# An attention and expert-routing layer on one core: the closing steps of the routing stage move from GpSimd to VectorE, and the closing orders of ScalarE and VectorE are written out

## What is computed

```python
x = x + layernorm(attn(layernorm(x)))     # linear attention: elu(q)+1, elu(k)+1, kv summed over the sequence
x = x + layernorm(ffn(layernorm(x)))

def _moe(x, wg, w1, v1, w2):
    scores = softmax(x @ wg.T)            # 32 experts
    weights, idx = top_k(scores, 8)
    weights = weights / sum(weights)
    # each token's row goes through 8 experts of width 192, and the results are added with their weights
    h = silu(xs @ w1[e]) * (xs @ v1[e])
    out = zeros.at[t_s].add((h @ w2[e]) * w_s)
```

## Time and profile before

| | us |
|---|---|
| median of 3 runs | 2469.23 (2468.17 to 2470.07) |
| profiled execution, its own time | 2465.01 |
| span of the profiled execution, first to last instruction | 2463.3 |
| PE busy in the span | 2234.5 (91%) |
| DVE busy | 1487.0 (60%) |
| ACT busy | 1237.6 (50%) |
| POOL busy | 956.6 (39%) |

### The profile page before, as it was taken

The page is one execution under the profiler, slowest core; times in us unless marked ns, Lnnn a source line. Parts: engine busy times, 40 slices in busy tenths (PEclk is TensorE's granted clock), DMA queues, the critical chain, the costliest instruction groups (busy, mean ns, idle before and its releaser), DMA issues.

```text
span 2463.3 us, 64597 instructions
## 1 busy us (share of the span) xinstructions
PE 2234.5 (91%) x11850; PEld 1922.4 (78%) x11851; DVE 1487.0 (60%) x4836; ACT 1237.6 (50%) x2643; POOL 956.6 (39%) x1128
## 2 busy tenths in 40 slices
PE   7999799999989999995698999989999898989980
PEld 5887488888858888884588988878889787978970
DVE  4555467777767777775555555565554555555546
ACT  3344456666655666663344454555444544454433
POOL 1212015555525555556333333333334333333432
PEclk9999899999999999997799999999999999999995
DMA  3234102333333333333897888888777777777767
GB/s 121 85 120 126 61 26 100 120 118 116 126 127 115 129 108 118 119 130 129 251 225 186 184 205 177 189 197 177 149 154 140 187 154 154 140 170 147 139 110 294
DMA packets 165230, 358.64 MB, mean 146 GB/s; under 512 B 21168, under 2 KB 21168, under 8 KB 165040
## 3 DMA queue, kind: packets, MB, share of 16 engines
q0 software_dynamic: 60512, 144.74, 28.4%
q1 hardware_dynamic: 91216, 173.89, 23.3%
q10 hardware_dynamic: 13440, 39.33, 4.8%
HBM read 178.21 MB, written 179.66 MB: 145 GB/s over the span
## 4 chain that ended last, share of the span: by engine, by line
PE 38%; issue 4%; DMA 3%; ACTq 3%; ACT 2%; DVE 1%; POOL 1%; DVEq 1%; SPq 0%; POOLq 0%
PE bank L465 7%; PE bank L467 6%; PE bank L466 6%; PE bank L456 4%; PE bank L482 3%; PE bank L486 2%; PE bank L475 2%; PE bank L484 2%; PE bank L483 2%; PE bank L485 2%; DMA LATE<-w_in 1%; DMA RAW<-w_in 1%; ACTq L325 1%; POOL sorted_rows L1525 1%; ACT WB L333 1%
## 5 line engine op out<-in xcount | busy, mean ns | idle before, releaser
L1459 POOL DMA_INDIRECT moe_sum<-Y,aidx x276 | 432.1, 1565 | 783.6 <-DMA moe_sum<-Y,aidx 404.0
L929 PE MATMUL bank<-WB,XH 128*128 128x512 f32 x1536 | 477.3, 392 | 0.0
L465 PE MATMUL bank<-WB,XL 128*128 x1104 | 399.5, 362 | 0.0
L467 PE MATMUL bank<-WB,XH 128*128 x1104 | 373.9, 339 | 0.0
L466 PE MATMUL bank<-WB,XH 128*128 x1104 | 372.3, 337 | 0.0
L929 PEld LDWEIGHTS bank<-WB,XH 128*128 128x128 f32 x1536 | 290.7, 189 | 58.3 <-issue 0.5
L929 PE MATMUL bank<-WB,XL 128*128 128x512 f32 x768 | 316.0, 411 | 10.4 <-DVE XL L1241 10.4
L929 PE MATMUL bank<-WB,SH 128*128 128x512 f32 x1024 | 317.3, 391 | 0.0
L709 DVE SCALAR_TENSOR_TENSOR BIG<-BIG,bank x276 | 95.9, 347 | 357.1 <-ACT BIG L527 270.5
L1525 POOL DMA_INDIRECT sorted_rows<-BIG,pos x256 | 265.7, 1038 | 94.6 <-issue 94.6
L527 ACT ACTIVATE BIG<-bank x276 | 91.4, 331 | 346.2 <-PE bank L467 320.3
(11 more groups left out here) (215 smaller groups left out, 4266.8 us busy)
## 6 DMA issues: line engine op xcount, KB each, us to landing
BIG<-sorted_rows SPq DMA_DIRECT2D x278, 274.0 KB
Y<-x_in SPq DMA_DIRECT2D x64, 256.0 KB, 2.8
RAW<-w_in ACTq DMA_DIRECT2D x15, 768.0 KB
LATE<-w_in ACTq DMA_DIRECT2D x15, 768.0 KB
sorted_rows<-BIG SPq DMA_DIRECT2D x33, 274.0 KB
moe_sum<-LATE SPq DMA_DIRECT2D x34, 256.0 KB, 3.0
LATE<-x_in SPq DMA_DIRECT2D x32, 256.0 KB
RAW<-wo_in SPq DMA_DIRECT2D x16, 512.0 KB, 3.5
```

The source lines that it names most:

```text
L465: nc.tensor.matmul(eu[s][:, 0:UP], XL[:, s, k, :], wh, start=k == 0, stop=False)
L467: last = nc.tensor.matmul(eu[s][:, 0:UP], XH[:, s, k, :], wl, start=False, stop=k == KC - 1)
L929: last = nc.tensor.matmul(ps, w, m, start=start and i == 0, stop=stop and i == len(terms) - 1)
L1459: nc.gpsimd.indirect_dma_start(acc_dram[:, :], bass.IndirectOffsetOnAxis(aidx[:, s:s + 1], 0), rows, None, compute_op=ALU.add).then_inc(s_ ...
```

## The change

GpSimd's list behind the last step of b keeps only the power -0.5 of each norm (`root`), the memory for padding (`set_pads`) and the scatters. VectorE does the rest: the residual adds and second norms of tiles 30 and 31, the output norm of tile 31, `pages_needed` for the tiles 29 to 31, and `note_pages` for the tiles 28 to 31. VectorE's and ScalarE's steps from step 32 (VectorE) and 33 (ScalarE) on are written out as `drain()`. Inside the loop nothing changes: there GpSimd still does all of it. `place` is cut in two, `place` and `place_rows`, so that in the closing steps `note_pages` can stand between them. The conversion of expert 0's weights moves: ScalarE's high parts stand behind tile 31's `turned`, and VectorE's low parts stand in `moe_dve`, behind the first part of the table. In `moe_act` the high parts of expert 1 now stand ahead of the load of expert 2.

```diff
+        def pages_needed(eng, t):
...
+            eng.tensor_scalar(need[:, :], carry[:, :], 0.0, None, ALU.is_gt).then_inc(s_need, 1)
+
+        def note_pages(eng, t, s):
...
@@ moe_act
             act.wait_ge(s_ex, TILES)
             nc.scalar.activation(negmax[:, :], mhalf[:, :], ACT.Silu)
+            for piece in range(len(PIECES)):
+                weights_high(act, 1, 1, 1, piece)
             act.wait_ge(s_elo, 1)
             load_weights(act, 2, 0)
-            for piece in range(len(PIECES)):
-                weights_high(act, 1, 1, 1, piece)
@@ moe_dve
             settled()
+            for piece in range(len(PIECES)):
+                weights_low(dve, 0, 0, 0, piece)
             steps = TILES // 4
             dve.wait_ge(s_pad0, 5)
             dve.wait_ge(s_pld, 16)
@@ ScalarE
+            def drain():
+                last = TILES - 1
+                turned(last - 1)
+                row_norm(last, 1)
+                exps(last - 1)
+                turned(last)
+                act.wait_ge(s_q, 4 * TILES)
+                for piece in range(len(PIECES)):
+                    weights_high(act, 0, 0, 0, piece)
+                exps(last)
+                row_out(last - 1, 0)
+                row_out(last, 1)
@@ VectorE
+            def rstd(slot, s_in, s_mid, s_out, n, s_used):
+
+                wait(dve, s_used, n - 1)
+                dve.wait_ge(s_in, n)
+                stand(dve)
+                nc.vector.tensor_scalar(ve[:, slot:slot + 1], mv[:, slot, 1:2], NORM_EPS, None, ALU.add).then_inc(s_mid, 1)
+                dve.wait_ge(s_mid, 2 * n)
+                stand(dve)
+                nc.vector.tensor_scalar(nmr[:, slot:slot + 1], mv[:, slot, 0:1], rs[:, slot:slot + 1], -1.0, ALU.mult,
+                                        ALU.mult).then_inc(s_out, 1)
+
+            def drain():
+                last = TILES - 1
+
+                def second_norm(t, s):
+                    dve.wait_ge(s_on, t + 1)
+                    dve.wait_ge(s_xres[s], (t - s) * 8 + 16)
+                    nc.vector.tensor_tensor(XRES[:, s, :], XRES[:, s, :], on, ALU.add).then_inc(s_x2, 1)
+                    dve.wait_ge(s_x2, t + 1)
+                    mean_var(XRES[:, s, :], 2, s_2bs, s_2mv, t + 1, s_2rs)
+                    rstd(2, s_2mv, s_2ve, s_2rs, t + 1, s_row)
+
+                def take_pages(t):
+                    ranks(t)
+                    pages_needed(dve, t)
+
+                def give_pages(t, s):
+                    place(t, s)
+                    note_pages(dve, t, s)
+                    last_pages(t)
+
+                def give_rows(t, s):
+                    place_rows(t, s)
+                    list_places(t, s)
+
+                scaled_low(4 * TILES - 2, 0)
+                list_places(last - 3, 0)
+                second_norm(last - 1, 0)
+                scaled_low(4 * TILES - 1, 1)
+                note_pages(dve, last - 3, 0)
+                last_pages(last - 3)
+                route(last - 2, 1)
+                take_pages(last - 2)
+                dve.wait_ge(s_o, 4 * TILES)
+                mean_var(po[1][:, :], 1, s_obs, s_omv, TILES, s_ors)
+                rstd(1, s_omv, s_ove, s_ors, TILES, s_on)
+                give_pages(last - 2, 1)
+                give_rows(last - 2, 1)
+                second_norm(last, 1)
+                route(last - 1, 0)
+                take_pages(last - 1)
+                give_pages(last - 1, 0)
+                give_rows(last - 1, 0)
+                route(last, 1)
+                take_pages(last)
+                give_pages(last, 1)
+                give_rows(last, 1)
@@ GpSimd
+            def root(slot, s_mid, n):
+                pool.wait_ge(s_mid, 2 * n - 1)
+                stand(pool)
+                nc.gpsimd.tensor_tensor(rs[:, slot:slot + 1], ve[:, slot:slot + 1], mhalf[:, :], ALU.pow).then_inc(s_mid, 1)
+
             def drain():
                 last = TILES - 1
-                residual(last - 1, 0)
-                rstd(2, s_2mv, s_2ve, s_2rs, last, s_row)
-                note_pages(last - 3, 0)
-                send(last - 3, 0, 0, 3)
-                pages_needed(last - 2)
-                rstd(1, s_omv, s_ove, s_ors, last + 1, s_on)
-                send(last - 3, 0, 3, 5)
-                residual(last, 1)
-                send(last - 3, 0, 5, 7)
-                rstd(2, s_2mv, s_2ve, s_2rs, last + 1, s_row)
-                note_pages(last - 2, 1)
-                send(last - 3, 0, 7, 8)
+                root(2, s_2ve, last)
+                send(last - 3, 0, 0, 5)
+                root(1, s_ove, TILES)
+                send(last - 3, 0, 5, TOP_K)
+                root(2, s_2ve, TILES)
                 set_pads()
-                send(last - 2, 1, 0, 2)
-                pages_needed(last - 1)
...
+                send(last - 2, 1, 0, TOP_K)
+                send(last - 1, 0, 0, TOP_K)
+                send(last, 1, 0, TOP_K)
```

More of the change, by code:

```diff
@@ L1153, in b_body @@
                     if c == 0 and live(t, 3):
[L1154 to L1161 removed]
+                        turned(t - 3)
                     if not fixed or 0 <= j - 2 < 4 * TILES:
@@ L1400, in b_body @@
             def b_body(t, s, b):
                 fixed = isinstance(t, int)
+                if fixed and t >= TILES:
+                    return
                 for c in range(CHUNKS):
@@ L1436, in b_body @@
                         route(t - 3, 1 - s)
-                    if fixed and (t, c) in FIRST_LOW:
-                        for piece in FIRST_LOW[t, c]:
-                            weights_low(dve, 0, 0, 0, piece)
                     if c == 3 and live(t, 3):
                         place(t - 3, 1 - s)
+                        place_rows(t - 3, 1 - s)
             run_b(dve, b_body)
+            drain()
             moe_dve(dve)
```

87 lines of the change are left out of this document (41 added, 46 removed).

## The result

The changed kernel took 2472.03 us in the median of 12 runs (2463.99 to 2479.78), beside 2464.62 for the kernel before (12 runs, 2457.00 to 2470.07). The ratio is 1.003, its 95% interval 1.0015 to 1.0044: 7.4 us, 0.3% slower, where 10.0 us faster (2459.2 us) was predicted, in a range that ended at 2467.5. The profiled execution took 2475.59 us, its span is 2473.3 us, 10.0 longer than before: 3.1 of them lie ahead of the closing steps, 4.1 in them and 2.8 behind them.

The account below looks back on a forecast made before the run. GpSimd's list in the closing steps was taken as the bound, with the table close behind. Earlier last scatter 8.1 plus landing 2.4 gave 10.5, less 0.5 for collisions: 10.0 us off 2469.2, so 2459.2 us, range 2454.5 to 2467.5.

Parts of the forecast that it names:

- the table chain: Closing steps, page list to table: list 11 us earlier, table 20.9 us behind it at 1180.9 or 1181.8, before the landing.
- a first transpose set free by the table: Sign of being wrong: TensorE's first expert transpose released by the table instead of by the scatters.
- the second rival: Closing steps: VectorE's two-input steps hold up GpSimd, or its handover chain becomes the bound; gain 0.9 us, 2468.3; chance 0.13.
- the room for tile 30: VectorE's chain: tile 30's positions ready near 1154, its scatters start at 1159.4, so 5 us of room.
- The slower rival: Experts' part: expert 2's load goes out late and ScalarE waits for it; 6 to 8.5 us slower, 2476; chance 0.05.
- the first rival: Closing steps: landing stays at 6.97 and the unexplained gap stays whole; gain 6.7 us, 2462.5; chance 0.18.
- First scatter: GpSimd's first scatter of tile 28 starts at 1133.0 instead of 1134.08, 1.1 us earlier.
- Stream: GpSimd, first to last scatter: pace 39.9, powers 1.8, padding 1.8, new wait 1.3, half the gap 0.9; 45.7 us.
- The unexplained gap: GpSimd, behind the first scatter: 2.11 us, 1.8 above the usual; half of that, 0.9, was taken to stay.
- Collisions: Closing steps: GpSimd slowed beside VectorE instructions with two SBUF inputs; 0.5 us put off the gain.
- Landing: Last scatter, start to landing: 4.6 us instead of 6.97 with one rival weight load less, 2.4 us gained.
- the case I had set beside the sum and not used: Last scatter: engines go round queues with work, so the landing stays near 6.97 and the sum is 8.1 us.

Follow-up runs that it names:

- e1: The changed kernel run again unaltered: 2454.47 us against 2463.50 for the kernel before, ratio 0.9973.
- e2: Changed kernel with expert 2's load ahead of the high parts of expert 1 again: 2456.17 us against 2463.50 for the kernel before, ratio 0.9981.
- e14: The changed kernel run again unaltered in a later set: 2462.59 us against 2465.05 for the kernel before, ratio 0.9995.
- e3: Changed kernel with VectorE's low parts of expert 0 ahead of tile 31's last row steps again: 2457.85 us against 2463.50 for the kernel before, 0.9979.
- e10: Changed kernel with expert 2's load issued only behind the first transposes: 2461.75 us against 2464.89 for the kernel before, 0.9989.
- e6: Changed kernel with both weight moves undone (expert 2's load, low parts of expert 0): 2454.91 us, 0.9946 of the kernel before.
- e4: Changed kernel with six GpSimd memsets as pauses between the scatters of tiles 29 to 31: 2458.75 us against 2463.50 for the kernel before, 0.998.
- e16: Changed kernel with six memsets of 0.5 us between the scatters of tiles 29 to 31: 2458.96 us against 2465.11 for the kernel before, 0.9974.
- e18: Changed kernel with the same six pauses between scatters, in another set: 2462.18 us against 2462.26 for the kernel before, 0.9993.
- e8: Changed kernel with only residual adds and linear norm steps back on GpSimd, page steps staying on VectorE: 2458.23 us, 0.997 of the kernel before.
- e7: Changed kernel with only the page steps back on GpSimd, adds and norm steps staying on VectorE: 2463.97 us, 0.9985 of the kernel before.
- e13: Changed kernel with expert 2's load behind the last scatters' landing and padding before tile 31's second power: 2462.53 us against 2465.05 for the kernel before, 0.9988.
- e9: Changed kernel with the padding ahead of GpSimd's power of tile 31's second norm: 2458.65 us against 2464.89 for the kernel before, 0.996.
- e12: The kernel before, profiled again to see how far stretches differ: last scatter +62.31, landing 7.24, transposes +76.62 us.

## Why the prediction was wrong, step by step

**Outcome.** The step that failed is the table chain: "Table 20.9 us behind the list", with VectorE's small steps priced at their own rows. In the first set VectorE's handovers to itself cost 17 us there: from the complete list (1165.03) to the written table (1200.77) it was 35.7 us, not 20.9. In e1 it was 19.5, and the table was written at +56.6, where the prediction had it. Without these waits the changed kernel's transposes start at +68.7 on average of five profiles. With them they start at +80.5, 11.8 later, more than the whole gain. The sum closes nearly: in the first trace SP's first row load (1202.16) follows 3.2 us behind VectorE's copy of the table (1198.97). In e1 that copy is at 1178.52, so the load could go at 1181.7, and it went at 1187.59, behind the scatters. The table had a cover of 5.9 us, and 17 less 5.9 is 11.1. That a first transpose set free by the table would be a sign of being wrong stood in the prediction, and the second rival named VectorE's chain with its handovers as a bound, but at no gain and by the room for tile 30, not as slower through single waits of 1 to 4 us. The slower rival (late load for expert 2) is refuted by e2 and by ScalarE's 0.76 of idle time at that conversion in the first trace. The gate was 4.1 us late in the one trace of the first set and the median 7.4, so 3 us of the median are not accounted for; whether all 12 runs had the waits isn't shown.

Where the waits lack, five sets are 4.2 to 10.0 us faster, 7.2 on average, near the 6.7 of the first rival and under the forecast's 7.7 to 14. That rival's two terms both came in the main: the gap stayed whole and the landing nearly so.

**First scatter:** predicted 1.1 earlier, measured 1.1 in all profiles of the changed kernel. (The steps listed for it add up to 1131.7, not to the 1131.9 written.) **Stream:** predicted 45.7 from first to last scatter, measured 46.3 to 46.9 (50.1 in e14, with GpSimd's break). That it came so near is in part luck, since terms that were off cancel. The unexplained gap stayed whole in every profile (2.15; I had taken half), the new wait for VectorE was 1.8 and not 1.3, but the two powers took 1.0 in sum and not 1.8, and the pace was 1.27 and not 1.287 (the seven intervals that I had averaged hold a scatter of 1.07). **Collisions:** the scatters keep 1.27 us beside VectorE's small routing steps, so the rival with 0.35 for each of 24 is refuted. Beside the low parts of expert 0, subtractions with two inputs in SBUF, they don't: 0.1 to 0.5 us more for each of two or three scatters, in e1 and in e3 alike. With the other long ones, scatters over 0.96 cost 1.2 us in e1's stream, where I had put 0.5.

**Landing:** predicted 4.6, measured 5.8 to 7.0, so 0.7 gained and not 2.4. My mechanism, one rival load less, was half right: e10 shows that expert 2's load is what holds the landing up, 2.84 without it. But its later issue didn't help (e6 has it 10 us earlier and a landing of 5.71). e4, e16 and e18 issue the last scatter 2 us later and land at the same +62 to +62.5, as if the engines by then work off a backlog. Busy time by stretch (columns as in the earlier trace rows), e1 and then e10, where the load is not there:

```profile
1180.00:1185.00 5.00, 0.00 (x0) 0.00 (x0) 4.38 (x11) 0.00 (x0) 0.15 (x1) 0.68 0.88 342
```

```profile
1180.00:1185.00 5.00, 0.00 (x0) 0.00 (x0) 4.46 (x12) 0.00 (x0) 0.00 (x0) 0.79 0.35 117
```

In e1 the engines still move 342 GB/s when GpSimd has issued everything (the last scatter starts at 1179.20).

The Trainium skill (DMA: Bandwidth & Descriptors, Queues, rings and completion order) has the engines go round the queues with work, which is the case I had set beside the sum and not used. By it alone the landing would have stayed near 6.97, and 5.8 to 7.0 was measured; e10, with that load's queue idle, agrees with it.

Together 1.1 + 6.0 + 0.7 is 7.8 us at the gate without the waits, what the transposes show (76.5 less 68.7), against 10.0 predicted.

**What made the gain:** e8 keeps 6.8 of the 7.8 us with the page steps alone, e7 none with adds and norms alone. I had costed both by GpSimd's time. That held for the page steps (and their handovers back and forth); an add taken off GpSimd only turned into GpSimd's wait for VectorE at the power.

**Room in VectorE's chain:** where no waits were, the page list was complete at +37.0 (predicted 35.7) and the table was written ahead of the landing. The low parts of expert 0 lay in the wait for the list and cost the table nothing, as predicted; what they cost the scatters stands above.

**What stays open** is the waits' cause. They are shown in the first set and on one of the six chips of the further sets, so the chip, or how the program came to lie on it, has a part. The kernel before had its usual times beside them (2464.6 and 2465.1), and its table had only 2 us of cover, so the changed order seems to have a part too; but no profile of the kernel before was taken beside e14. That the unbroken row of scatters brings them on is argued from how they end in e13 and e14, behind breaks of 3.88 and 5.15 us; that they outlast a break of 1.29 and the last scatter in the first trace speaks against its simplest form. That SP and GpSimd were late too says that the cause isn't in VectorE alone. The pair that was to test it twice met no such chip.

## What to carry to other kernels

Taking small steps off the engine that feeds a transfer stream pays only while that engine is the bound: here, with the steps off, moving the last issue by another 1 to 2.5 us either way no longer changed when it landed, while taking away the bulk load beside it did. A chain of many tiny instructions that hand over to each other has a risk that its rows don't show: a cover of 5.9 us ahead of the landing was enough in five sets and 11 us short in the first, so a verdict under 1% wants sets on several chips. Where two kinds of step move together, undo each alone: here one made nearly all of the gain and the other alone none.

## What the runs showed of the hardware

VectorE's wait for its own previous result, 0.11 us or less at the same places in e1, took up to 4.06 us beside scatters that kept their pace of 1.27 us, in two of seven sets. An indirect scatter of GpSimd takes 0.96 us of issuing, and 1.23 to 1.47 beside VectorE's subtractions with two inputs in SBUF (e1, e3). Beside GpSimd's memset of 128x1240 VectorE's add of 128x512 took 1.60 us instead of 0.68 (e9). The landing of the last scatter took 2.84 us without a weight load beside it (e10) and 4.6 to 7.2 with one (e4, e12). The experts' part of the very same kernel took 1256.6 to 1271.0 us in five profiles, far more than anything in the closing steps.
